# Four-head attention over image rows: products with x on 128 partitions, another order of each row's TensorE work, exponentials scaled by GpSimd, two of four heads turned in transpose mode

## The reference, cut to what matters

```python
x = _layernorm(pair_rep, gamma, beta)
q = x @ Wq * C ** (-0.5)           # 4 heads of 32 numbers, per row s of the image
k = x @ Wk
v = x @ Wv
dpa = jnp.einsum('nsqhc,nsvhc->nsqvh', k, q)
pair_bias = x @ Wb
attention = jax.nn.softmax(dpa + bias + pair_bias[:, None], axis=3)
out = jnp.einsum('nsqvh,nsvhc->nsqhc', attention, v)
fu = jax.nn.sigmoid(x @ Wu + bu)
out = (out * fu).reshape(n, s, s, H * C) @ Wo + bo
out = out * mask[..., None]
```

## Time and profile before

| | |
|---|---|
| median of three runs | 2724.7 us (2724.25 to 2729.43) |
| the profiled execution, its own time | 2724.38 us |
| its span | 2722.6 us |
| PE busy over the span | 2412.6 us (89%) |
| DVE, ACT, POOL busy | 2180.0, 1798.4, 1940.2 us |
| loop over image rows, first to last score product (L468) | 80.2 to 529.4 us |

### The profile page before, as it was taken

How to read it: one execution, slowest core, us unless ns; L and a number is a source line. 1 busy time by engine, 2 the same in 40 slices (tenths; PEclk the granted TensorE clock), 3 DMA queues, 4 the chain that set the end, 5 groups by cost and what they waited for, 6 DMA issues and landing times. The chain is left out here.

```text
span 2722.6 us, 40183 instructions
## 1 busy us (share of the span) xinstructions
PE 2412.6 (89%) x10620; PEld 1195.4 (44%) x10620; DVE 2180.0 (80%) x2229; ACT 1798.4 (66%) x4094; POOL 1940.2 (71%) x1197
## 2 busy tenths in 40 slices
PE   6999999857459899999999999999999999998587
PEld 6577667624324334434433433333333333333533
DVE  4455555560639999999999999999999999998766
ACT  4688778743657778878877875665566556653376
POOL 3900000030239999999999999999999999999379
PEclk7799999969679999999999999999999999999799
DMA  3000000000146767676666767777777677775022
GB/s 66 11 10 10 10 8 9 7 1 0 43 130 222 220 227 228 223 230 220 229 228 221 234 226 250 243 237 235 238 247 238 225 235 246 239 223 189 3 62 62
DMA packets 186408, 421.08 MB, mean 155 GB/s; under 512 B 66548, under 2 KB 87513, under 8 KB 186330
## 3 DMA queue, kind: packets, MB, share of 16 engines
q1 hardware_dynamic: 184794, 416.01, 48.1%
q10 hardware_dynamic: 1536, 4.20, 0.5%
HBM read 387.63 MB, written 24.12 MB: 151 GB/s over the span
## 5 line engine op out<-in xcount | busy, mean ns | idle before, releaser
L1553 POOL TENSOR_TENSOR s_hc<-s_h,s_cc 128x1024 f32<-128x1024 f32 x512 | 1201.2, 2364 | 62.9 <-PE s_py L1316 44.5
L1316 PE MATMUL s_py<-s_hc,ident 128*128 128x512 f32 x2048 | 1019.0, 623 | 8.6 <-DVE s_yo L1598 8.6
L1635 DVE TENSOR_TENSOR_SCAN s_h<-s_dA,s_state,s_pu 128x1024 f32<-128x1024 f32 x330 | 770.4, 2342 | 29.5 <-PE s_pu L1294 6.1
L1316 PEld LDWEIGHTS s_py<-s_hc,ident 128*128 128x128 f32 x2048 | 365.1, 194 | 456.1 <-issue 419.3
L1469 ACT ACTIVATE s_dA<-s_dt,ss_A 128x1024 f32<-128x1024 f32 x352 | 401.7, 1142 | 9.1 <-ACT s_brow L1432 7.7
L1474 ACT ACTIVATE s_pu<-s_dt,ss_A 128x1024 f32<-128x1024 f32 x160 | 178.4, 1115 | 319.1 <-DVE s_h L1635 313.9
L1546 POOL TENSOR_TENSOR s_dbx<-s_dtx,s_bb 128x1024 f32<-128x1024 f32 x160 | 378.0, 2363 | 7.4 <-DMA s_bb<-rows_scratch 7.4
L1611 DVE TENSOR_TENSOR s_pu<-s_pu,s_dtx 128x1024 f32<-128x1024 f32 x288 | 349.7, 1214 | 24.5 <-PE s_pu L1303 24.5
L1635 DVE TENSOR_TENSOR_SCAN s_h<-s_pu,s_state,s_dbx 128x1024 f32<-128x1024 f32 x150 | 350.2, 2335 | 16.8 <-ACT s_pu L1474 16.6
L234 POOL MEMSET rn_n_add<- 128x1 f32 x1 | 0.1, 103 | 403.9 <-POOLq L78 403.9
L1303 PE MATMUL s_pu<-s_bcs,ss_sel 48*128 48x512 bf16 x576 | 175.2, 385 | 92.4 <-DVE s_h L1635 92.3
(11 more groups left out here) (267 smaller groups left out, 3700.6 us busy)
## 6 DMA issues: line engine op xcount, KB each, us to landing
s_cc<-rows_scratch SPq DMA_DIRECT2D x512, 512.0 KB, 4.6
s_bb<-rows_scratch SPq DMA_DIRECT2D x160, 512.0 KB, 5.0
s_n<-n_scratch SPq DMA_DIRECT2D x64, 258.0 KB, 5.6
y_scratch<-s_yo SPq DMA_DIRECT2D x16, 512.0 KB, 5.4
s_yf<-y_scratch SPq DMA_DIRECT2D x16, 512.0 KB, 6.4
x_tok<-in_x_dram SPq DMA_DIRECT2D x16, 256.0 KB, 4.5
at_xg<-at_xT SPq DMA_DIRECT2D x64, 64.0 KB, 2.0
n_scratch<-ss_turned SPq DMA_DIRECT2D x32, 128.0 KB, 2.3
```

Of the source, the lines that this page charges most:

```text
L1316: ins = nc.tensor.matmul(p_y[:, hf], lhsT=c.ident[:, :], rhs=hc[:, s % RING, hf], start=(s == 0), stop=(s == U - 1))
L1553: nc.gpsimd.tensor_tensor(hc[:, s % RING, :], h[:, s % RING, :], cc[:, s % C_RING, :], ALU.mult).then_inc(read, 1)
L1635: nc.vector.tensor_tensor_scan(out=flow(h[:, s % RING, :]), data0=flow(decays), data1=flow(inputs), initial=begun, op0=ALU.mult, op1=ALU.a ...
```

## The change

- The weights `at_wq`, `at_wk`, `at_wvu` get 128 partitions, the upper half filled with zeros (the bias row `bu` stays in partition 64 of `at_wvu`), and all four products with x contract over 128 partitions.
- PE's order in a step becomes: scores of row r, attention product of row r-4, turning of row r-3, values of row r, projection, output product of row r-5. The output product writes to the bank `ar_pso` beside the attention product, where before it wrote to `ar_pss`; it waits for the gate of the row behind it (`gated`), and the attention product waits until x has been added to (`x_done`).
- The reciprocal sums are not spread by PE any more. POOL multiplies the exponentials with them, 128 by 512 numbers in place (`even_out`), between DVE's reciprocal and PE's turning. DVE's multiplication L550 goes.
- Heads 1 and 3 are turned by `nc.tensor.transpose`, heads 0 and 2 by a product with the identity as before.
- Buffers grow (`ar_ex`, `ar_tot`, `ar_rs` to four rows, `ar_va` to eight), and each row goes through one more step.

```diff
-LAG = 5
+LAG = 6
...
-        wq, wk = sb("at_wq", [D, 128]), sb("at_wk", [D, 128])
-        wvu = sb("at_wvu", [D + 1, 256])
+        wq, wk = sb("at_wq", [128, 128]), sb("at_wk", [128, 128])
+        wvu = sb("at_wvu", [128, 256])
...
-                pool.wait_ge(padded, 3)
+                for w in (wq, wk, wvu):
+                    nc.gpsimd.memset(w[D:128, :], 0.0).then_inc(padded, 1)
+                pool.wait_ge(padded, 6)
...
-                nc.tensor.matmul(ps_p[:, :], lhsT=wq[:, :], rhs=xg[0:D, k, :], start=True, stop=True).then_inc(q_made, 1)
+                nc.tensor.matmul(ps_p[:, :], lhsT=wq[:, :], rhs=xg[:, k, :], start=True, stop=True).then_inc(q_made, 1)
...
-            def project_output(r, j):
-                pe.wait_ge(scaled, r + 1)
+            def project_output(r, j, next_attended):
+                pe.wait_ge(gated, r + 2 if next_attended else r + 1)
                 need(pe, x_done, r)
-                nc.tensor.matmul(p_y, lhsT=og2[:, j % 2, :], rhs=wo[:, :], start=True, stop=True).then_inc(y_made, 1)
+                nc.tensor.matmul(p_y, lhsT=og[:, j % 2, :], rhs=wo[:, :], start=True, stop=True).then_inc(y_made, 1)
...
             def turn(r, j):
-                pe.wait_ge(exped, r + 1)
+                pe.wait_ge(evened, r + 1)
                 need(pe, e_taken, r)
                 for h in range(HEADS):
-                    ins = nc.tensor.matmul(ps_t[:, tile(h)], lhsT=ex[:, j % 2, h, :], rhs=c.ident[:, :],
-                                           start=True, stop=True)
+                    if h % 2:
+                        ins = nc.tensor.transpose(ps_t[:, tile(h)], ex[:, j, h, :], c.ident[:, :])
+                    else:
+                        ins = nc.tensor.matmul(ps_t[:, tile(h)], lhsT=ex[:, j, h, :], rhs=c.ident[:, :],
+                                               start=True, stop=True)
...
-            def attend(r, j):
+            def attend(r, j, k):
                 pe.wait_ge(e_taken, r + 1)
                 pe.wait_ge(v_taken, r + 1)
-                pe.wait_ge(inverted, r + 1)
-                need(pe, scaled, r)
+                need(pe, gated, r)
+                need(pe, x_done, r - 1)
                 for h in range(HEADS):
-                    nc.tensor.matmul(ps_o[band[h], 0:128], lhsT=va[:, j, band[h]], rhs=exT[:, j % 2, tile(h)],
-                                     start=True, stop=True)
-                for h in range(HEADS):
-                    ins = nc.tensor.matmul(ps_o[band[h], 128:256], lhsT=rs[:, j % 2, h:h + 1].to_broadcast([128, HC]),
-                                           rhs=c.ident[:, :], start=True, stop=True)
+                    ins = nc.tensor.matmul(ps_o[band[h], 0:128], lhsT=va[:, k, j, band[h]], rhs=exT[:, j % 2, tile(h)],
+                                           start=True, stop=True)
...
+            def even_out(r, j):
+                pool.wait_ge(inverted, r + 1)
+                by_head = rs[:, j, :].rearrange("p (h a) -> p h a", a=1).to_broadcast([128, HEADS, 128])
+                nc.gpsimd.tensor_tensor(ex[:, j, :, :], ex[:, j, :, :], by_head, ALU.mult).then_inc(evened, 1)
+
             def group(g):
                 for j in range(GR):
                     scale_bias(g * GR + j, j)
-                for j in range(GR):
+                    even_out(g * GR + j, j)
                     add_output_bias(g * GR + j, j)
```

More of the change, by code:

```diff
@@ L286, in load_weights @@
             n = 0
-            for dst, src in ((wq[:, :], A["Wq"]), (wk[:, :], A["Wk"]), (wvu[0:D, 0:128], A["Wv"]),
+            for dst, src in ((wq[0:D, :], A["Wq"]), (wk[0:D, :], A["Wk"]), (wvu[0:D, 0:128], A["Wv"]),
                              (wvu[0:D, 128:256], A["Wu"]), (wvu[D:D + 1, 128:256], row_of(A["bu"])),
@@ L501, in step @@
                     need(pe, added, r)
[L502 to L505, removed]
                     score(r, j, g, k)
-                if has(2):
-                    turn(r - 2, (j - 2) % GR)
+                if has(4):
+                    attend(r - 4, j, 1 - k)
                 if has(3):
-                    attend(r - 3, (j - 3) % GR)
+                    turn(r - 3, (j - 3) % GR)
                 if has(0):
@@ L519, in step @@
                         project_u(g + 1, 1 - k)
+                if has(5):
+                    project_output(r - 5, (j - 5) % GR, has(4))
             project_q(0, 0, 0)
@@ L537, in invert_sums @@
                 dve.wait_ge(exped, r + 1)
-                need(dve, o_made, r - 1)
-                nc.vector.reciprocal(rs[:, j % 2, :], tot[:, j % 2, :]).then_inc(inverted, 1)
+                need(dve, evened, r - GR + 1)
+                nc.vector.reciprocal(rs[:, j, :], tot[:, j, :]).then_inc(inverted, 1)
             def apply_gate(r, j, g, k):
@@ L559, in step @@
             def step(r, j, g, k, has, pair):
+                if has(6):
+                    add_to_x(r - 6)
                 if has(0):
                     add_bias(r, j)
-                if has(5):
-                    add_to_x(r - 5)
+                if has(4):
+                    apply_gate(r - 4, j, g - 1, 1 - k)
                 if has(2):
                     invert_sums(r - 2, (j - 2) % GR)
-                if has(3):
-                    apply_gate(r - 3, (j - 3) % GR, g if j == 3 else g - 1, k if j == 3 else 1 - k)
                 if has(0):
                     minimum(r, j)
-                if has(3):
-                    normalise(r - 3, (j - 3) % GR)
             row_steps(dve, step)
@@ L624, in exponentiate @@
                 act.wait_ge(least, r + 1)
-                need(act, e_turned, r - 1)
-                need(act, inverted, r - 1)
+                need(act, e_turned, r - GR + 1)
+                need(act, inverted, r - GR + 1)
                 for h in range(HEADS):
-                    ins = nc.scalar.activation(ex[:, j % 2, h, :], sc[:, j, h, :], ACT.Exp, bias=mn[:, j, h:h + 1],
-                                               scale=-1.0, accum_out=tot[:, j % 2, h:h + 1])
+                    ins = nc.scalar.activation(ex[:, j, h, :], sc[:, j, h, :], ACT.Exp, bias=mn[:, j, h:h + 1],
+                                               scale=-1.0, accum_out=tot[:, j, h:h + 1])
                 ins.then_inc(exped, 1)
@@ L640, in step @@
                     take_k(g + 1, 1 - k)
-                if has(2):
-                    take_turned(r - 2, (j - 2) % GR)
+                if has(3):
+                    take_turned(r - 3, (j - 3) % GR)
                 if has(0):
-                    take_values(r, j)
+                    take_values(r, j, k)
             take_q(0, 0)
```

38 lines of the change are left out of this document (16 added, 22 removed).

## The result

The changed kernel takes 2647.9 us (median of 4 runs, 2637.3 to 2649.3) against 2725.5 us before (4 runs, 2724.3 to 2729.4): 0.971 of the time, 95% interval 0.969 to 0.973. The profiled execution took 2649.26 us, its span 2647.5 us, 75.1 us less than before.

A forecast was written before the change was run, and what follows sets the result against it. PE was taken as the loop's bound: four steps from 14.08 to 11.84 us, 30.5 groups, 68.3 us; plus 1 us for first steps, less 0.5 for memsets, 68.8 off 2724.38 gives 2655 us; range 2637 to 2693.

The forecast's parts named there:

- Spread reciprocals: PE's step in the image-row loop: L494, spreading the reciprocals, goes and takes 0.24 us off.
- Changes of shape: PE's step with a projection: operand shape changes fall from five to three, 0.10 us each, 0.20 us off a step.
- Transposes: PE's turning: two heads by transpose (0.23 us) and two by product (0.50 us) make 0.73 us.
- First rival: PE's turning: alternating products and transposes costs mode changes, so the transposes save nothing; 2692 to 2704 us; chance 0.16.
- The wait for the x addition: PE's attention product waits for DVE's addition to x: 0.13 us a step, bounds nothing to 0.25 us.
- The sum: Loop on PE: steps of 3.18 and 2.30 us, 11.84 us for four against 14.08; 68.8 us off in all.
- POOL is covered: POOL's multiplication, 1.34 us, ends before PE's turning needs it, by 1.0 us or 0.15 us; POOL does not bind.
- Second rival: POOL takes 2.7 us, every turning waits, 12.9 us a group, 35 us saved: 2689 us; chance 0.06.
- ACT as the next bound: Loop: ACT's work is 11.37 us for four steps, 4% under PE's 11.84, so it binds next.
- First steps: The first five loop steps, at the 1.2 GHz level, were taken to gain 1 us.
- third rival: More gain: the DVE wait is hidden, groups fall to 11.4 us, earlier clock adds up to 7: 2635 to 2643; chance 0.10.
- The clock, rival at 0.04: Granted clock does not hold with PE's less dense list: 22.8 us a group, 2992 us over the whole stage; chance 0.04.

The follow-up runs named there:

- the order alone: Changed kernel with x products back on 64 partitions and all four heads turned by products, keeping new order, longer lag and POOL's scaling: 2783.7 us median (2733 to 2938).
- the early one: Changed kernel with the output product moved ahead of the values product, all else the same: 2635.1 us, ratio 0.970.

## Why the prediction was right

It forecast 2655 us and 68.8 us of gain; 2647.9 us came. The bound, the mechanism and the likeliest case were right, but two sizes inside the sum were wrong, each by 0.19 us a step, and cancelled. That is luck: without it the forecast would have been 23 us off either way.

- **Spread reciprocals, 0.24 us.** As forecast, though no kernel leaves them out alone: against 0.32 us of wait it makes the 0.31 us that four steps of the order alone are longer.
- **Changes of shape, 0.10 us each: too small by half.** The term was read from the piece ahead of the change alone (0.34 against 0.24 us). The piece behind pays as much: 0.19 us a change in the kernel before with 128 partitions (four steps 0.78 us shorter for one change), in the new order (14.40 to 12.84 for two) and with the values on 64 partitions (1.54 for two). Two changes were worth 0.39 us a step, not 0.20.
- **Transposes, 0.27 us a step: 0.23.** First rival refuted.
- **The wait for the x addition, 0.13 us: 0.32.** It lay outside its stated bounds. The step that failed was where the output product ends: 0.07 us behind the scores' start by its busy time, and DVE 0.07 us later. DVE started at 0.32. The end that the view shows for a product doesn't say when the next engine may start: behind the scores DVE started 0.07 us after it, behind the output product 0.25 us after it (251.55 to 251.80). Why these differ is open. The latency back to PE (0.15) was right.
- **The sum.** 0.24, 0.39 and 0.23 us off and 0.32 on are 0.54 us of a long step of 3.74, and it became 3.22. The parts, read from other kernels and from the timeline, add up.
- **POOL is covered:** right, with 1.04 us instead of 1.34. PE waited for it twice, 0.4 us in total. Second rival refuted. Its price had been added up wrongly: steps of 4.4 + 2.3 and 4.4 + 1.4 us are 12.5 us for a group, not 12.9, and so some 48 us saved, not 35.
- **ACT as the next bound at 11.37 us:** wrong in size, 10.4; durations were added where starts are closer together. It did not touch the forecast, as PE was the bound at 11.93, but it hid that two more transposes would pay in full.
- **First steps, 1 us: 8.6,** since the clock rose at about 84 us and not at 100. The prediction had this only in its third rival, with up to 7 us. The loop gave 66.9 us for 68.3. Ahead of it 2.0 us were gained where 0.5 us of loss was forecast; the first score product of the 14 profiled executions lies anywhere between 71 and 80 us, so these 2.0 us are put down to no edit. The end of the stage and the later layers lost 2.4 us where nothing was forecast. Together this is the 6.3 us between the forecast 68.8 and the 75.1 us of the profiled execution.
- **The clock, rival at 0.04.** In the changed kernel it holds. But the prediction weighed the zero-filled partitions as a matter of shapes, with one clause on how they fill the array. Without them the same kernel runs at half clock and takes 2982 us. In this kernel they are not worth 0.39 us a step but 334 us.

## What to carry over

When PE is the bound, count changes of operand shape (partitions contracted by columns out) in its order and price each by the pieces on both sides; put products of one shape side by side even if one must be padded with zeros. Look at the granted clock of every variant, also where PE is busy without a gap: less work on PE can go with half the clock. Before moving a product behind which another engine works, follow the waits on both sides: the late output product made PE wait for the addition to x, the early one stands right behind the gate.

## What the runs showed of the hardware that was not expected

- PE busy for 150 of 150 us is no sign of the upper clock: with x products on 64 partitions in the new order the granted clock stayed at 0.50 for nearly 700 us, with the output product late or early, and with products instead of transposes it lay between in three of four executions (means 0.854 to 0.927). The old order with 64 partitions and two transposes kept 1.00 in the loop (2693 us). With the three projections on 128 partitions it was 1.00 in every variant profiled. It also rose early there: in these nine kernels, one profiled execution each, it reached 1.00 between 71 and 91 us. In the five with all products with x on 64 partitions it was 98 us once, 100 us twice, and twice it didn't in the loop. What exactly decides it was not settled: a kernel with filler products in place of the zeros was not run.
- Transposes do not pull the clock down by themselves: with products with x on 128 partitions all four heads in transpose mode ran at 1.00. With those on 64 partitions two transposes in place of two products went with the lower clock in all four executions. The Trainium skill (TensorE: Matmul & The Clock Gate, Part 4: PE-mode transpose) says that the upper clock does not engage for this mode; here, among products on 128 partitions, it was held and the kernel had the lowest median of all.
- A product over 65 partitions changes shape like one over 128: in the kernel before, in the step with the gate's projection (65 partitions), the values take 0.42 us and not 0.32, and the output product 0.26 us and not 0.37, so the change stands in front of the projection and not behind it:

```profile
307.70 0.48 PE L474 MATMUL ar_psv<-at_wvu,at_xg 64*128 64x128 f32 x2
308.12 1.13 PE L457 MATMUL ar_psp<-at_xg,at_wvu 65*128 65x512 f32 x2
309.08 0.33 PE L463 MATMUL ar_pss<-at_wo,ar_og 128*128 128x64 f32 x2
309.34 0.50 PE L468 MATMUL ar_pss<-ar_qT,ar_kT 32*128 32x128 f32 x8
```

- In the kernel with four transposes two ACT copies out of PSUM that follow each other start 0.48 us apart, though the first is shown as 0.59 us long.
